# First layer by rows: weights of a two-part MLP kernel in strips of two chunks from two queues, and twelve warm-up multiplications

## The reference

```python
h = jax.nn.gelu(jnp.einsum('bnd,hd->bnh', x, fc1_w) + fc1_b, approximate=False)   # HID = 1024
shared = jnp.einsum('bnh,sh->bns', h, fc2_w) + fc2_b                              # 192 features
We = experts_w[indices]
be = experts_b[indices]
expert_x = jnp.einsum('bnh,bph->bnp', h, We) + be[:, None, :]                     # 64 features
return x + jnp.concatenate([shared, expert_x], axis=-1)
```

## Time and profile before

| | us |
|---|---|
| median of 3 runs | 363.93 (363.26 to 364.14) |
| the profiled execution's own time | 363.34 |
| its span, first to last instruction | 361.5 |

### The profile page before, as it was taken

One profiled execution on the slowest core, in us unless ns is written; L12 is line 12 of the kernel. 1 busy time (PEld: TensorE's weight loads), 2 busy tenths in 40 slices (PEclk: granted clock), 3 DMA queues, 4 the chain that ended last, 5 costly groups with the idle time before them and its releaser, 6 DMA issues.

```text
span 361.5 us, 7842 instructions
## 1 busy us (share of the span) xinstructions
PE 356.4 (99%) x2863; PEld 350.3 (97%) x2863; DVE 224.0 (62%) x367; ACT 243.6 (67%) x410; POOL 222.2 (61%) x100
## 2 busy tenths in 40 slices
PE   8999999999999999999999999999999999999996
PEld 6898999999999999999999999999999999999996
DVE  1797993937758285683937658395673938653241
ACT  3794865757849576694857759576794857757560
POOL 0079824676655677565676655677565577655381
PEclk9999999999999999999999999999999999999999
DMA  8869856361703426044261603526052321403011
GB/s 202 183 160 117 156 143 150 126 160 45 175 22 116 127 69 173 31 124 89 82 160 52 168 25 109 132 82 162 29 140 74 94 91 58 126 18 100 2 58 58
DMA packets 70447, 37.86 MB, mean 105 GB/s; under 512 B 43530, under 2 KB 70410, under 8 KB 70410
## 3 DMA queue, kind: packets, MB, share of 16 engines
q1 hardware_dynamic: 69792, 36.85, 40.8%
q10 hardware_dynamic: 618, 0.53, 0.6%
HBM read 28.97 MB, written 8.39 MB: 103 GB/s over the span
## 4 chain that ended last, share of the span: by engine, by line
PE 95%; issue 2%; POOL 1%; ACT 1%; DVE 0%; POOLq 0%
PE fc_ps L985 37%; PE acc_ps L1017 16%; PE acc_ps L1021 16%; PE acc_ps L1019 16%; PE fc_ps L961 6%; PE fc_ps L930 1%; POOL ht L353 1%; PE tr_ps L924 1%; PE fc_ps L968 1%; ACT ht L510 0%; ACT gelu L536 0%; DVE work L794 0%; DVE resid L819 0%; ACT w1t L430 0%; PE acc_ps L924 0%
## 5 line engine op out<-in xcount | busy, mean ns | idle before, releaser
L353 POOL TENSOR_TENSOR ht<-gelu,ht 128x1024 fp32r<-128x1024 f32 x60 | 144.5, 2408 | 121.3 <-ACT ht L510 121.3
L985 PE MATMUL fc_ps<-xt,w1t 128*128 128x256 f32 x1176 | 173.2, 283 | 0.0
L985 PEld LDWEIGHTS fc_ps<-xt,w1t 128*128 128x128 f32 x1176 | 155.3, 192 | 0.1
L1017 PE MATMUL acc_ps<-w2t,ht 128*128 128x256 f32 x512 | 144.9, 283 | 0.2 <-POOL ht L353 0.2
L1019 PE MATMUL acc_ps<-w2t,ht 128*128 128x256 f32 x512 | 144.9, 283 | 0.0
L1021 PE MATMUL acc_ps<-w2t,ht 128*128 128x256 f32 x512 | 144.9, 283 | 0.0
L1017 PEld LDWEIGHTS acc_ps<-w2t,ht 128*128 128x128 f32 x512 | 98.3, 192 | 0.6 <-POOL ht L353 0.3
L1019 PEld LDWEIGHTS acc_ps<-w2t,ht 128*128 128x128 f32 x512 | 98.3, 192 | 0.3
L1021 PEld LDWEIGHTS acc_ps<-w2t,ht 128*128 128x128 f32 x512 | 98.3, 192 | 0.0
L510 ACT ACTIVATE ht<-gelu 128x1024 fp32r<-128x1024 f32 x64 | 68.0, 1062 | 3.3
L496 ACT ACTIVATE work<-fc_ps 128x512 f32<-128x512 f32 x28 | 16.8, 600 | 57.4 <-PE fc_ps L985 57.4
(11 more groups left out here) (57 smaller groups left out, 279.5 us busy)
## 6 DMA issues: line engine op xcount, KB each, us to landing
pieces<-in_L_cond_experts_w SPq DMA_DIRECT2D x128, 64.0 KB, 2.0
out<-resid SPq DMA_DIRECT2D x32, 256.0 KB, 3.0
pieces<-in_x SPq DMA_DIRECT2D x60, 128.0 KB, 3.6
resid<-in_x SPq DMA_DIRECT2D x15, 512.0 KB, 4.1
bias<-in_L_cond_experts_b SPq DMA_DIRECT2D x32, 32.0 KB, 2.9
w_piece<-in_L_cond_fc_w SPq DMA_DIRECT2D x4, 256.0 KB, 4.5
w_piece<-in_L_cond_fc_w SPq DMA_DIRECT2D x4, 192.0 KB, 5.0
resid<-in_x SPq DMA_DIRECT2D x2, 256.0 KB, 3.4
```

Source lines behind the costliest of these rows:

```text
L353: nc.gpsimd.tensor_tensor(ht[:, slot, LO, :, :].rearrange("p k t -> p (k t)"), gelu[:, q % GELUS, :, :].rearrange("p k t -> p (k t)"), ht[ ...
L985: last = nc.tensor.matmul(fc1_ps[:, dst, j * SEQ:(j + 1) * SEQ], w1t[:, w, wv, ms], xt[:, n % 2, o, xv, :], start=(fresh and j == 0 and at ...
L1017: nc.tensor.matmul(dst, h_hi_t, w_hi, start=(r == 0 and u % (2 * T) == 0), stop=True, skip_group_check=True)
```

## The change

Block 0's first work is cut by rows of the block (b = 0, 1), and fc1's first half of weights by pairs of hidden chunks (l = 0: chunks 0 and 1; l = 1: chunks 2 and 3).

- DMAs: `load_w1_pair(queue, l)` loads two chunks in four DMAs of 64 KB. ACT's queue now issues only pair 0, without the index ahead of it. SP issues pair 1, b1 and the index behind the two DMAs of x, and only then waits for `x0_loaded[0]` and goes on with chunks 4 to 7.
- PE: 12 warm-ups and none later; x of row 0, weights of pair 0, x of row 1 are transposed (4 each); then `first_chunk(c, b)` multiplies chunk c for the 256 tokens of row b. Chunks 0 and 1 are done for row 0, pair 1 is transposed, and chunks 0 and 1 are done for row 1. Twelve multiplications of 512 columns become 24 of 256.
- ACT and DVE: x and weight banks alternate; on ACT gelu of chunk 1 now stands ahead of the last `w1_high`; on DVE the b1 copy still follows `w1_low` number 2.
- A bank now holds both feature chunks of two hidden chunks, or of one row of x, so that the copies write with other strides; their sizes stay 512 columns.

The diff, cut to its core:

```diff
-    WARM = 20
+    WARM = 12
...
-        def load_w1(queue, half):
-            ks = slice(half * HALF, (half + 1) * HALF)
+        def load_w1_pair(queue, l):
             for q in range(Q):
-                queue.dma_start(w1_in[S * q:S * (q + 1), ks, :], w1_v[q][:, ks, :])\
-                    .then_inc(w1_loaded[half], 16)
+                queue.dma_start(w1_in[S * q:S * (q + 1), 2 * l:2 * l + 2, :],
+                                w1_v[q][:, 2 * l:2 * l + 2, :]).then_inc(w1_loaded[l], 16)
...
+            load_w1_pair(sp, 1)
+            sp.dma_start(b1_in[:, :].rearrange("k (q c) -> k q c", q=Q),
+                         fc1_b.rearrange("(q k c) -> k q c", q=Q, c=S))\
+                .then_inc(b1_loaded, 16)
+            sp.dma_start(index_sb[:, :], index.rearrange("(o n) -> o n", o=1))\
+                .then_inc(index_loaded, 16)
             sp.wait_ge(x0_loaded[0], 16)
-            load_w1(sp, 1)
+            for q in range(Q):
+                sp.dma_start(w1_in[S * q:S * (q + 1), HALF:K, :], w1_v[q][:, HALF:K, :])\
+                    .then_inc(w1_loaded[2], 16)
...
-            act.dma_start(index_sb[:, :], index.rearrange("(o n) -> o n", o=1))\
-                .then_inc(index_loaded, 16)
-            load_w1(act, 0)
-            act.dma_start(b1_in[:, :].rearrange("k (q c) -> k q c", q=Q),
-                          fc1_b.rearrange("(q k c) -> k q c", q=Q, c=S))\
-                .then_inc(b1_loaded, 16)
+            load_w1_pair(act, 0)
...
-            for d in range(D):
-                x0_high(d)
-            for d in range(D):
-                w1_high(0, d)
+            x0_high(0)
+            w1_high(0, 0)
+            x0_high(1)
+            w1_high(0, 1)
             act.wait_ge(b1_ready, 1)
             conv_chunk(0)
             w1_high(1, 0)
+            conv_chunk(1)
             w1_high(1, 1)
-            conv_chunk(1)
...
+            def first_chunk(c, b):
+                for at, (w, v, d) in enumerate([(w, v, d) for w, v in ((HI, HI), (HI, LO), (LO, HI))
+                                                for d in range(D)]):
+                    if c == 0 and at == 0:
+                        pe.wait_ge(w1_hi, 1)
+                        pe.wait_ge(x0_hi, b + 1)
+                    if c == 0 and (w, v, d) == (HI, LO, 0):
+                        pe.wait_ge(x0_lo, b + 1)
+                    if c == 0 and (w, v, d) == (LO, HI, 0):
+                        pe.wait_ge(w1_lo, 1)
+                    last = nc.tensor.matmul(fc1_ps[:, c, b * SEQ:(b + 1) * SEQ],
+                                            conv_operand(c, d, w),
+                                            xt0[:, d, v, b * SEQ:(b + 1) * SEQ],
+                                            start=(b == 0 and at == 0), stop=True,
+                                            skip_group_check=True)
+                if b == R - 1:
+                    last.then_inc(conv_filled, 1)
...
-            for b in range(R):
-                x0_banks(b)
-            warm(WARM // 2)
+            x0_banks(0)
             pe.wait_ge(w1_loaded[0], 16 * Q)
-            for d in range(D):
-                w1_bank(0, d)
+            w1_bank(0, 0)
+            x0_banks(1)
+            first_chunk(0, 0)
             pe.wait_ge(b1_loaded, 16)
             nc.tensor.transpose(fc1_ps[:, 3, 0:K], b1_in[:, :], ident[0:K, 0:K]).then_inc(b1_tr, 1)
-            first_chunk()
+            first_chunk(1, 0)
             pe.wait_ge(w1_loaded[1], 16 * Q)
-            for d in range(D):
-                pe.wait_ge(x0_lo, d + 1)
-                w1_bank(1, d)
-            conv_chunk(1)
+            w1_bank(0, 1)
+            first_chunk(0, 1)
+            first_chunk(1, 1)
+            pe.wait_ge(w1_loaded[2], 16 * Q)
+            pe.wait_ge(x0_lo, 1)
+            w1_bank(1, 0)
+            pe.wait_ge(x0_lo, 2)
+            w1_bank(1, 1)
+            pe.wait_ge(w1_lo, 2)
             conv_chunk(2)
             conv_chunk(3)
-            pe.wait_ge(w1_lo, 4)
+            pe.wait_ge(w1_lo, 3)
             conv_chunk(4)
             conv_chunk(5)
+            pe.wait_ge(w1_lo, 4)
             conv_chunk(6)
             conv_chunk(7)
```

More of the change, by code:

```diff
@@ L113, in cond_mlp_residual, with x0_row, x0_bank, w1_slots @@
         xt0 = xt_plain[0]
+        def x0_row(v, b):
+            return xt0[:, :, v, b * SEQ:(b + 1) * SEQ]
+        def x0_bank(b):
+            return tr_ps[:, b, :].rearrange("p (d t) -> p d t", d=D)
+        W1_ORDER = ((0, 1), (1, 0))
+        def w1_slots(half, l, v):
+            cols = slice(2 * half * P, (2 * half + 2) * P)
+            if l == 0:
+                return w1t[:, W_A11:W_A12 + 1, v, cols]
+            return w1t[:, W_A22:W_A21 + 1:W_A21 - W_A22, v, cols]
+        def w1_rows(half, l):
+            return (acc_ps, tr_ps)[half][:, l, :].rearrange("p (d c) -> p d c", d=D)
         x0_loaded = [sem(f"x0_loaded{b}") for b in range(R)]
@@ L120, in cond_mlp_residual @@
         stored = [sem(f"stored{n}") for n in range(2)]
-        w1_loaded = [sem(f"w1_loaded{n}") for n in range(2)]
+        w1_loaded = [sem(f"w1_loaded{n}") for n in range(3)]
         w1p_loaded = sem("w1p_loaded")
@@ L414, in _, with x0_high, w1_high @@
         def _(act):
[L415 to L430, removed]
+            def x0_high(b):
+                act.wait_ge(x0_tr, b + 1)
+                nc.scalar.activation(x0_row(HI, b), x0_bank(b), ACT.Copy).then_inc(x0_hi, 1)
+            def w1_high(half, l):
+                act.wait_ge(w1_tr, 2 * half + l + 1)
+                nc.scalar.activation(w1_slots(half, l, HI), w1_rows(half, l), ACT.Copy)\
+                    .then_inc(w1_hi, 1)
             def s_high(s):
@@ L643, in _, with x0_low, w1_low @@
         def _(dve):
[L644 to L660, removed]
+            def x0_low(b):
+                dve.wait_ge(x0_hi, b + 1)
+                nc.vector.tensor_tensor(x0_row(LO, b), x0_bank(b), x0_row(HI, b).bitcast(FP32),
+                                        ALU.subtract).then_inc(x0_lo, 1)
+            def w1_low(half, l):
+                dve.wait_ge(w1_hi, 2 * half + l + 1)
+                nc.vector.tensor_tensor(w1_slots(half, l, LO), w1_rows(half, l),
+                                        w1_slots(half, l, HI).bitcast(FP32), ALU.subtract)\
                     .then_inc(w1_lo, 1)
@@ L819, in drain @@
                     nc.vector.tensor_tensor(dst, src, dst, ALU.add).then_inc(drained, 1)
-            for d in range(D):
-                x0_low(d)
-            for d in range(D):
-                w1_low(0, d)
+            x0_low(0)
+            w1_low(0, 0)
+            x0_low(1)
+            w1_low(0, 1)
             dve.wait_ge(b1_tr, 1)
             nc.vector.tensor_copy(b1[:, :], fc1_ps[:, 3, 0:K]).then_inc(b1_ready, 1)
-            for d in range(D):
-                w1_low(1, d)
+            w1_low(1, 0)
+            w1_low(1, 1)
             w2_square(0)
@@ L934, in x0_banks, with w1_bank @@
                 pe.wait_ge(x0_loaded[b], 16)
[L935 to L945, removed]
+                transposes(tr_ps[:, b, :], [
+                    feature_chunk(resid[:, 0, b * T + t, :], d)
+                    for d in range(D) for t in range(T)]).then_inc(x0_tr, 1)
+            def w1_bank(half, l):
+                k = half * HALF + 2 * l
+                transposes((acc_ps, tr_ps)[half][:, l, :], [
+                    feature_chunk(w1_in[:, k + j, :], d)
+                    for d in W1_ORDER[l] for j in range(2)]).then_inc(w1_tr, 1)
             def conv_operand(j, d, v):
```

## The result

The changed kernel takes 365.97 us (median of 5, 364.49 to 366.16), the kernel before beside it 364.14 (363.26 to 364.24). The ratio is 1.0043, 95% interval 1.0028 to 1.0058: slower by 0.4%, and outside the range that I had given. Its five runs form two groups, 364.5 and 364.7, and 366.0 to 366.2.

A forecast was written before the change was run, and what follows sets the result against it. PE, 95% of the chain, was taken to bound the kernel, with POOL's first piece holding fc2's first unit. 363.34 - 0.04 gave 363.3, with 0.59 to the median 363.9, taken as 363.8 us; range 363.0 to 365.2.

The forecast's parts named there:

- That PE's lead becomes a wait in front of fc2: PE ends chunk 7 near 19.3, 1.9 us ahead of before, then waits about 1.5 for POOL's first piece.
- W: Start of DVE's first `w2_square`, its first transpose of fc2's weights; forecast 13.45 us, against 13.21 before.
- The prediction's own sign of being wrong: POOL's first piece moves by over 0.5 us either way, or another wait stands behind fc2's first unit.
- The way from the weight transposes to W: From PE's first weight transposes through DVE and ACT to DVE's first transpose of fc2's weights: 8.35 us.
- T: Start of pair 1's transposes on PE, put 3.2 us after the first weight transposes' load starts.
- the gelu ahead of the last copy: On ACT, gelu of chunk 1 moved ahead of the last weight copy; claimed to cost 0.50 us.
- S = 5.1: Start of the first weight transposes' load on PE, forecast at 5.1 us, bounds 4.6 to 5.75.
- pair 0 at 4.8: Landing of the first weight pair from ACT's queue, forecast at 4.8 us, bounds 4.3 and 5.75.
- 13.49 - 14.61: Gain at fc2's first multiplication, written as 13.49 - W; forecast 0.04 us.
- Rival 3: Pair 0 lands late as two streams share the first half megabyte: 0.6 us more, 364.5; chance 0.12.
- rival 1: PE stays at 1.2 GHz through first transposes and multiplications: 1.5 us more, 365.4; chance 0.16.
- the 0.59: Median 363.93 lies 0.59 us above the profiled execution's 363.34; added at the end of the sum.
- Edits at nothing: Half multiplications, b1 and index DMAs on SP, ACT's shorter queue and strided copies counted as costing nothing.

The follow-up runs named there:

- Experiment 4: `conv_high_early`: changed kernel with ACT's HI part of the first hidden pair moved ahead of the copies of fc2's weights; 365.65 us, ratio 1.0049.
- the order experiments: Changed kernel with PE, ACT and DVE work behind pair 1 reordered, without and with five warm-ups in PE's gap; 364.51 us (ratio 1.0026) and 364.37 (1.0013).
- experiment 3: `gelu_back`: changed kernel with ACT's earlier order, both weight copies of chunks 4 to 7 ahead of gelu of chunk 1; 365.14 us, ratio 1.0039.
- experiment 9: `half_load`: changed kernel with loads by pairs undone, ACT's queue loading chunks 0 to 3 in four DMAs of 128 KB; 366.77 us, ratio 1.0063.
- `fill5`: Changed kernel with five warm-ups put between the transposes of x of row 0 and the first weight transposes; 364.89 us, ratio 1.0028.
- `after_resid`: Changed kernel with POOL's bias addition to block 1 of x held until DVE's last two LO pieces of that block; 365.62 us, ratio 1.0029.
- `order`: Changed kernel with PE, ACT and DVE work behind pair 1 reordered, PE's gap left unfilled; 364.51 us, ratio 1.0026.
- the three with the fill: Reordered changed kernel with five warm-ups in the gap: alone 364.37 us; with POOL's block 1 addition held back 363.67; with pair 0 issued from both queues 365.56.
- `split_pair0`: Changed kernel with pair 0's strips issued from both queues, 0 and 1 by ACT, 2 and 3 by SP between x's DMAs; 365.57 us, ratio 1.0046.
- `before_warm12`: Kernel before with twelve warm-ups at the start and none later, nothing else changed; 363.91 us, ratio 0.9994.
- `order_fill_split`: Changed kernel reordered behind pair 1, with five warm-ups in the gap and pair 0's strips issued from both queues; 365.56 us, ratio 1.0054.

## Why the prediction was wrong

*That PE's lead becomes a wait in front of fc2*: right, and the heart of it. POOL's piece, ACT's list and DVE's W were the right places; 7.36 from W to POOL was measured as 7.33. The prediction's own sign of being wrong came all the same: POOL's first piece ends at 21.94 instead of the 20.81 forecast. Experiment 4 adds that POOL isn't alone there: two more results of DVE stand just behind.

*The way from the weight transposes to W* (8.35): measured 8.57. `w1_lo` came at S + 2.11, as predicted; from there to the start of chunk 1, two multiplications and the b1 transpose took 0.64 instead of 0.38, which makes T = S + 3.47. Gelu of chunk 0 followed 2.21 behind T (the terms written add up to 2.18, not to 2.23) and W 2.89 behind gelu. This way is the change's own cost: before it was 13.21 - 7.43 = 5.8, and the order experiments brought it back to 6.8. The b1 copy behind pair 1 and the gelu ahead of the last copy are in it as predicted (0.5, experiment 3).

*S = 5.1*: this step failed first. I took pair 0 at 4.8 from an even share of the bytes, with bounds 4.3 and 5.75. It landed at 6.0, outside both. The sum has no term for the issues: four of them took 0.45 each, as the larger ones did, so that the last strip was issued at 2.18, and its landing took 3.8. Rival 3 had a late pair 0 at 0.12, through shared bytes, and too small. How much of the 3.8 is due to the bytes ahead stays open; experiment 9 shows that bytes count too: with 256 KB more behind the same four issues of this queue, the transposes started 0.93 later in its profile. The late S explains the profiled pair, 364.49 against 363.34: 0.94 of lateness and 0.22 on the way give W at 14.61, and 13.49 - 14.61 = -1.12, against the 1.15 measured. Two more profiles with a quick chunk 0 follow the same line: the transposes start at 6.42 in `fill5` and 6.61 in `after_resid`, W is 8.56 and 8.55 behind them, and the executions took 364.87 and 365.05. So a landing that varies from run to run is part of the spread.

*The clock*: this step decides the median. I gave rival 1 a chance of 0.16 with 1.5 us more, 365.4; three of five runs are in that group, and seven of the twelve of `after_resid` lie above 365.5. The rival was weighed wrongly: I took the forecast from one quick execution and even took 0.1 off the 0.59 that lies between it and the median, with the reason that fewer warm-ups leave less to stretch. The opposite holds. With the gap, the rise came late in `conv_high_early`, which costs 1.04 on the way to W, and the grant was lost again in `half_load`, which costs 2.45 (11.02 - 8.57). From the profiled 364.49 to the median 365.97 it is 1.48: a late rise is 1.04 of that, and a later landing (0.4 and 0.6 in the two profiles above) or a lost grant can be the rest, which no profile of that execution splits.

That the upper group is the clock is shown by `fill5`: it gives PE idle work in the gap, changes no load, and removes the group. The mean granted clock of each run, taken over its whole span, supports it. The median run itself has 0.994, the only one of the five below 1.00. Of the 48 runs of kernels with the unfilled gap (the changed kernel, `after_resid`, `gelu_back`, `conv_high_early`, `order`, `half_load`) twelve have 0.995 or less; of the 36 with five warm-ups in it none has less than 0.998. A late first rise doesn't show in this number, since the column reads 1.00 there too: for the runs at 366.10 and 366.16, both 1.00, the slow multiplications are read from a sibling's profile, not from their own.

The rule cited with rival 1, of the Trainium skill (TensorE: Matmul & The Clock Gate, Part 4: PE-mode transpose), that transposes don't engage the full clock, is neither borne out nor refuted. With transposes and a gap behind twelve warm-ups, chunk 0 was multiplied quickly from 7.48 on in the changed kernel and slowly from 8.35 to 9.9 in `conv_high_early`; with five warm-ups between them it was quick in each of four profiles (`fill5` and the three with the fill). With smaller gaps (0.26 and 0.54) the two cases differ as well: behind twelve warm-ups and twelve transposes chunk 0 was quick in `split_pair0` (1.23 from 7.20), and behind sixteen transposes most of it was slow in `before_warm12`.

The step "Edits at nothing" has an error that cost nothing here. It lets the queued transfers cover the later issue of fc2's weights. They were issued 0.5 later, the last at 7.6 instead of 7.1, and the longest landing was 5.5 as before, so that they can be as late as 13.1 and not 12.6. With W at 14.61 DVE didn't wait for them; in `order_fill_split` it did.

## What to carry to other kernels

Before an engine is made earlier, follow the first unit that it will meet, and then the next two results behind it. Here the experts' LO part was ready at 21.3, POOL's piece at 21.94 and x's LO part at 24.94, 0.05 ahead of PE, and only shortening the way to their common start W moved the time. Splitting a load into halves halved no issue time here; for the first operands count issues as well as bytes. The gap on TensorE in the first microseconds was paid twice, as waiting and in the clock, so fill such a gap with work that nothing waits for. Judge a start-up by many runs, since one profile shows one of them only. And give a repair that helps both kernels to both, before the gain is put down to the change.

## What the runs showed of the hardware

- Two of DVE's pieces of 1024 columns took 1.5 us more when a POOL addition of 1024 columns (2.42) overlapped them for 1.8: 4.00 instead of 2.47. With POOL held back until they were done, the two took 1.21 and 1.23.
- The granted clock can fall again after it has risen: 1.00, then 0.52 and 0.51 over 7 us, behind an idle stretch of 1.77 us in PE's first eight (`half_load`); the multiplications of 256 columns then took 415 ns (median) instead of 282.
- Five warm-ups in that gap cut the spread of the changed kernel's times from 1.7 us (5 runs) to 0.6 (8 runs).
- DMAs of fc1's and fc2's weights of 64, 128 and 192 KB, on 32 partitions each, took 0.43 to 0.45 us to issue (medians).
